# Second attention of a two-layer gated block: scores from the raw context through folded query-key weights, two query tiles on the row halves of TensorE

## What is computed

```python
q = jnp.einsum('bld,de->ble', query, Wq) + bq      # query: 4 x 256 x 128, layer-normalised x
k = jnp.einsum('bld,de->ble', key, Wk) + bk        # key = ctx_512: 4 x 512 x 64, Wk: 64 x 128
v = jnp.einsum('bld,de->ble', value, Wv) + bv      # value = ctx_512
scores = jnp.einsum('bqe,bke->bqk', q, k)
attn = jax.nn.softmax(scores, axis=-1)
out = jnp.einsum('bqk,bke->bqe', attn, v)
...
x = x + jnp.tanh(g_xattn[1]) * out
x = x + jnp.tanh(g_ffn[1]) * _L1_ffn_ref(_layernorm(x, axis=-1), ...)
```

## Time and profile before

| what | value |
|---|---|
| median of the three timed runs | 331.62 us |
| time of the profiled execution | 333.15 us |
| its span | 331.4 us |
| PE busy | 314.9 us, 95% |
| DVE, ACT, POOL busy | 220.3, 193.9, 115.4 us |
| PE's share of the chain that ended last | 74% |

### The profile page before, as it was taken

One profiled execution on the slowest core, in us unless ns is written; L12 is line 12 of the kernel. 1 busy time (PEld: TensorE's weight loads), 2 busy tenths in 40 slices (PEclk: granted clock), 3 DMA queues, 4 the chain that ended last, 5 costly groups with the idle time before them and its releaser, 6 DMA issues.

```text
span 331.4 us, 7484 instructions
## 1 busy us (share of the span) xinstructions
PE 314.9 (95%) x2899; PEld 189.5 (57%) x2899; DVE 220.3 (66%) x531; ACT 193.9 (59%) x410; POOL 115.4 (35%) x200
## 2 busy tenths in 40 slices
PE   8999999999999999899989999999997999999995
PEld 3545734344444434344577677777894467676665
DVE  4998899898989889676352143332322857679665
ACT  3468588989988898787368533333346356422221
POOL 6376723246334333231685004434342301110000
PEclk9999999999999999999999799999999999999999
DMA  7956994661337006150351580000003000000101
GB/s 173 213 106 163 178 211 115 141 168 52 135 115 209 5 3 193 52 146 2 92 179 36 140 212 11 26 13 28 15 18 113 25 2 0 3 0 0 32 3 32
DMA packets 35827, 27.83 MB, mean 84 GB/s; under 512 B 5627, under 2 KB 33070, under 8 KB 35792
## 3 DMA queue, kind: packets, MB, share of 16 engines
q1 hardware_dynamic: 33965, 25.04, 29.6%
q0 software_dynamic: 1280, 1.88, 1.8%
q10 hardware_dynamic: 547, 0.44, 0.5%
HBM read 11.89 MB, written 5.26 MB: 52 GB/s over the span
## 4 chain that ended last, share of the span: by engine, by line
PE 74%; ACT 6%; DVE 6%; POOL 5%; issue 4%; DMA 2%; SPq 1%; DVEq 0%; POOLq 0%; ACTq 0%
PE psum L1881 12%; PE psum L1683 12%; PE psum L1962 8%; PE psum L1624 5%; PE psum L1648 5%; PE psum L1950 4%; PE psum L1869 4%; ACT qk_r L949 2%; POOL rows_in L798 2%; PE psum L1651 2%; PE psum L2065 2%; PE psum L2057 1%; ACT parts L949 1%; PE psum L1701 1%; PE psum L1819 1%
## 5 line engine op out<-in xcount | busy, mean ns | idle before, releaser
L1212 DVE TENSOR_REDUCE nmax<-psum 128x2 f32<-128x1024 f32 (+2 forms) x88 | 101.9, 1214 | 11.0 <-PE psum L1624 9.7
L949 ACT ACTIVATE parts<-psum 128x512 f32<-128x512 f32 (+1 forms) x88 | 45.2, 566 | 8.6 <-PE psum L1648 7.7
L1881 PE MATMUL psum<-p_more,kcat 128*128 128x320 f32 (+2 forms) x160 | 41.9, 408 | 0.9 <-DVE p_more L1345 0.7
L820 POOL DMA_INDIRECT rows_back<-qcat,back_at x24 | 22.9, 953 | 47.8 <-ACT qcat L982 41.8
L1881 PEld LDWEIGHTS psum<-p_more,kcat 128*128 128x128 f32 x160 | 26.9, 195 | 9.9 <-issue 2.2
L1349 DVE TENSOR_TENSOR qcat<-psum,qk_r 128x320 f32<-128x320 f32 (+2 forms) x40 | 16.7, 422 | 22.8 <-ACT qk_r L990 22.7
L990 ACT ACTIVATE qk_r<-psum 128x320 f32<-128x320 f32 (+2 forms) x40 | 15.3, 384 | 25.6 <-PE psum L1881 24.3
L1683 PE MATMUL psum<-parts,v_aug 128*18 128x256 f32 (+1 forms) x352 | 28.5, 369 | 0.0
L1962 PE MATMUL psum<-h_t,kcat 128*128 128x512 f32 x60 | 28.1, 594 | 0.0
L1683 PE MATMUL psum<-qk_r,v_aug 128*18 128x256 f32 (+1 forms) x160 | 27.4, 373 | 0.0
L1028 ACT ACTIVATE qk_r<-psum 128x512 f32<-128x512 f32 x15 | 9.0, 597 | 30.1 <-PE psum L1962 30.1
(11 more groups left out here) (248 smaller groups left out, 621.4 us busy)
## 6 DMA issues: line engine op xcount, KB each, us to landing
kcat<-parts SPq DMA_DIRECT2D x18, 192.0 KB, 3.8
qcat<-parts SPq DMA_DIRECT2D x21, 128.0 KB, 3.7
kcat<-ones_b SPq DMA_DIRECT2D x8, 192.0 KB, 4.0
kcat<-in_L_ffn_wi_gate_dram SPq DMA_DIRECT2D x6, 256.0 KB, 4.2
kcat<-in_L_ffn_wi_up_dram SPq DMA_DIRECT2D x6, 256.0 KB, 4.5
kcat<-in_L_ffn_wo_dram SPq DMA_DIRECT2D x6, 256.0 KB, 5.7
parts<-in_L_ffn_w_dram SPq DMA_DIRECT2D x3, 512.0 KB, 5.5
rows_in<-zeros SPq DMA_DIRECT2D x1, 1290.0 KB, 6.0
```

Source lines behind the costliest of these rows:

```text
L820: pool.indirect_dma_start(out=rows_back[:, :], out_offset=bass.IndirectOffsetOnAxis(ap=back_at[0:m, e, t:t + 1], axis=0), in_=eo[0:m, e % ...
L949: act.activation(p_slots[u % NPT][:, 0:w], s2_bank(s2_place[u])[:, 0:w], ACT.Exp, scale=SCALE).then_inc(p_in, 1)
L1212: dve.tensor_reduce(dst[:, :, n * g:n * (g + 1)], src.rearrange("p (r q k) -> p r q k", r=PAR, q=n), AX.X, ALU.max, negate=True).then_inc( ...
L1881: ins = pe.matmul(gate_up_bank(i, m)[:, 0:end - first], w_t[e][:, m, f * P:(f + 1) * P], xs_t[:, e % 2, first:end], start=True, stop=True)
```

## The change

The scores are no longer made from keys. With `M = Wq Wk'` (128 x 64) a score is `(x M + Wk bq)` times the raw context row, plus an offset `x Wq bk + bq bk` that is the same for a whole row of scores. The row offset does not alter the softmax, but the kernel does keep it: it goes through the DVE step that makes the exponential's bias. The values are computed as they were. What the edit does, in the order of the program:

- the four key products and their four ACT copies are gone; PE turns `w1_q` and `w1_k`, ACT copies the result, PE makes `mk` (the folded 64 columns, one column of query bias for each half of the partitions, one offset column), ACT copies it; the value products stand around these; eight `unread` products follow them, and three more follow the first turn of the routed experts' rows
- SP copies `c_t` from partitions 0-63 to 64-127 (512 KB), behind the loads of the experts' rows and ahead of the loads of layer 1's expert weights
- queries are made 64 wide, an even tile on partitions 0-63 and an odd one on 64-127; one product of 128 by 1 per tile makes the offsets
- the scores of a batch's two tiles are two products of 64 rows, one on each half of the array, issued together; the loop goes by batch and no longer by tile
- DVE has one more small instruction behind each maximum, in two of the steps it waits for the offsets; ACT has three small copies more
- after the first scores three `unread` products stand ahead of the transposes

```diff
-        c_t = sb("c_t", [DC + 1, NC * P])
+        c_t = sb("c_t", [P, NC * P])
...
-        k1_t = q_place(AFTER_HH + 6 * D, NC * P)
+        AFTER_EO = AFTER_HH + 6 * D
+        w1_turned = q_place(AFTER_EO, D + DC + 1)
+        bq_wide = q_place(AFTER_EO + 256, D)
+        MK_BIAS, MK_OFF = DC + 1, DC + 2
+        mk = q_place(AFTER_EO + 384, MK_OFF + 1)
...
+            sp.wait_ge(kv1_full, B)
+            sp.dma_start(c_t[DC:2 * DC, :], c_t[0:DC, :]).then_inc(ctx_again, 16)
...
             def max1(t):
                 dve.wait_ge(sc1_full, t + 1)
-                dve.tensor_reduce(s1_nmax[:, t:t + 1], bank(t % 2), AX.X, ALU.max, negate=True).then_inc(nm1_in, 1)
+                link(dve.tensor_reduce(s1_nmax[:, t:t + 1], bank(t % 2), AX.X, ALU.max, negate=True))
+                if t in (first for first, _ in BACK):
+                    dve.wait_ge(off1_in, [first for first, _ in BACK].index(t) + 1)
+                dve.scalar_tensor_tensor(out=s1_bias[:, t:t + 1], in0=s1_nmax[:, t:t + 1], scalar=s1_off[:, t:t + 1],
+                                         in1=s1_off[:, t:t + 1], op0=ALU.subtract, op1=ALU.add).then_inc(nm1_in, 1)
...
+            def fold_weights_qk():
+
+                pe.wait_ge(mk_act, 1)
+                pe.wait_ge(bq_in, 1)
+                pe.wait_ge(wt_in[0], W_LAST[MK_BANK] + 1)
+                wq, wk, dst = w1_turned[:, 0:D], w1_turned[:, D:D + DC + 1], bank(MK_BANK)
+                pe.matmul(dst[:, 0:DC + 1], wq, wk, start=True, stop=True)
+                for t in range(QT):
+                    pe.matmul(dst[t * DC:(t + 1) * DC, MK_BIAS:MK_BIAS + 1], wk[:, 0:DC], b1_col[:, :], start=True, stop=True)
+                pe.matmul(dst[:, MK_OFF:MK_OFF + 1], bq_wide, wk[:, DC:DC + 1], start=True, stop=True).then_inc(mk_full, 1)
...
-            for j in range(2 * B):
-                context(j)
+            turn_weights_qk()
+            context(0)
+            fold_weights_qk()
+            for b in range(1, B):
+                context(b)
+            unread(N_UNREAD_ROWS)
...
-                pe.matmul(bank(Q1_BANK)[:, 0:(end - first) * P], w1_q[:, :], h_t[:, first * P:end * P],
-                          start=True, stop=True).then_inc(q1_full, 1)
-
-            def scores1(t):
-                pe.wait_ge(q1_act, next(s + 1 for s, (first, end) in enumerate(BACK) if t < end))
+                for t in range(first, end):
+                    dst = bank(Q1_BANK)[t % QT * DC:(t % QT + 1) * DC, (t - first) // QT * P:((t - first) // QT + 1) * P]
+                    ins = pe.matmul(dst, mk[:, 0:DC], h_t[:, t * P:(t + 1) * P], start=True, stop=True)
+                ins.then_inc(q1_full, 1)
+
+            def offsets1(s):
+                first, end = BACK[s]
+                if s == 0:
+                    pe.wait_ge(wt_in[1], E)
+                for t in range(first, end):
+                    ins = pe.matmul(bank(OFF1_BANK[s])[:, t - first:t - first + 1], h_t[:, t * P:(t + 1) * P], mk[:, DC:DC + 1],
+                                    start=True, stop=True)
+                ins.then_inc(off1_full, 1)
+
+            def scores1(b):
+                pe.wait_ge(q1_act, next(s + 1 for s, (first, end) in enumerate(BACK) if QT * b < end))
+                if b == 0:
+                    pe.wait_ge(ctx_again, 16)
+                else:
+                    pe.wait_ge(p1_in, QT * b)
+                for t in range(QT * b, QT * b + QT):
+                    half = slice(t % QT * DC, (t % QT + 1) * DC)
+                    pe.matmul(bank(t % 2), q1_t[half, b, :], c_t[half, b * SC:(b + 1) * SC],
+                              start=True, stop=True).then_inc(sc1_full, 1)
```

More of the change, by code:

```diff
@@ L219, in flamingo_gated_kernel @@
         v1 = q_place(AFTER_HH + 6 * D + NC * P, NC * D).rearrange("p (t d) -> p t d", t=NC)
-        q1_t = qk[:, :, SC:SC + BANK]
-        def q1_of(first, end):
-            return q1_t[:, first // (BANK // P), first % (BANK // P) * P:first % (BANK // P) * P + (end - first) * P]
+        q1_t = qk[:, 0, SC:SC + B * P].rearrange("p (b q) -> p b q", b=B)
         raw1 = raw1_f.rearrange("p (e m d) -> p e m d", e=E, m=3)
@@ L1498, in _ @@
             statistics(2, 2, x_sb)
[L1499 to L1507, removed]
+            max1(1)
+            normalise(2, 2, x_sb)
+            for b in range(B):
+                if b + 1 < B:
+                    max1(QT * (b + 1))
+                    max1(QT * (b + 1) + 1)
+                if b == 2:
                     normalise(3, 0, x1_sb)
-            add_values(NT - 1)
+                reciprocal1(b)
+                add_values(QT * b)
+                add_values(QT * b + 1)
             dense_experts()
@@ L1919, in routed_experts @@
                 transpose_rows(0)
+                unread(N_UNREAD_FIRST)
                 for e in range(E - 1):
@@ L2016, in _, with unread, turn_weights_qk @@
-            for j in range(2 * B):
-                context(j)
+            def unread(n, place=0):
+                for _ in range(n):
+                    pe.matmul(bank(place), ones_b[:, 0:P], ones_b[:, 0:BANK], start=True, stop=True)
+            def turn_weights_qk():
+                dst = bank(TURN1_BANK)
+                pe.transpose(dst[:, 0:D], w1_q[:, :], ident[:, :])
+                pe.transpose(dst[:, D:D + DC + 1], w1_k[:, :], ident[0:DC + 1, 0:DC + 1]).then_inc(mk_full, 1)
+            def fold_weights_qk():
[7 more added lines that the diff above has]
+                pe.matmul(dst[:, MK_OFF:MK_OFF + 1], bq_wide, wk[:, DC:DC + 1], start=True, stop=True).then_inc(mk_full, 1)
@@ new lines, in context @@
+            def context(b):
+                if b == B - 1:
+                    pe.wait_ge(kv1_act, 1)
+                else:
+                    pe.wait_ge(wt_in[0], W_LAST[V1_BANK[b]] + 1)
+                for c in range(CT):
+                    tok = (CT * b + c) * P
+                    ins = pe.matmul(bank(V1_BANK[b])[:, c * P:(c + 1) * P], c_t[0:DC + 1, tok:tok + P], w1_v[:, :],
+                                    start=True, stop=True)
+                ins.then_inc(kv1_full, 1)
+            turn_weights_qk()
@@ L2028, in turn_weights1 @@
                 ins.then_inc(tr_full[1], 1)
-            def unread(n):
-                for _ in range(n):
-                    pe.matmul(bank(0), ones_b[:, 0:P], ones_b[:, 0:BANK], start=True, stop=True)
             def turn_back(s):
```

148 lines of the change are left out of this document (87 added, 61 removed).

## The result

The changed kernel is slower: median 333.52 us (22 runs, 331.57 to 335.60) against 331.84 us (22 runs) for the kernel before timed beside it, ratio 1.005 with a 95% interval of 1.003 to 1.007. The forecast was 331.3 us, and 333.52 lies outside its range.

A forecast was written before the change was run, and what follows sets the result against it. PE was taken to bound most of the chain, with the first expert's row load arriving alongside it in the context stage. Context stage 0 and second attention -0.3 from the 331.62 us median gave 331.3 us, range 329.4 to 332.8.

The forecast's parts named there:

- The context stage: PE work up to the first expert's rows: 3.48 us removed, 3.57 added, so gain 0, at best 0.2 us.
- The reading of the median: Clock fall ahead of the experts, 1.73 us in the profiled run before, does not happen in a typical run.
- E: Rival: clock falls in the new gap behind the second attention's first scores, up to 1.7 us more, 333.0 us; chance 0.09.
- B: Rival: the median run holds the context-stage clock fall and the change removes it, 1.7 us less, 329.6 us; chance 0.27.
- C: Rival: second attention's offset products nearly free, or a wait shorter than read, 0.7 us less, 330.6 us; chance 0.10.
- D: Rival: 32-bit score products on row halves do not overlap, 1.74 us a pair, 1.5 us more, 332.8 us; chance 0.10.
- The walk of the second attention: Step-by-step timing from first scores to dense units: 0.25, say 0.3 us gained, with 0.6 us doubt either way.
- the period: Second attention's loop per batch: set by latency, 4.29 us against 4.40 before, with PE idle 0.5 us a batch.
- the tail: End of the second attention: dense units start 6.65 us after the last batch's scores.
- The DVE step: Second attention: an added instruction between each tile's maximum and exponential, 0.20 us each.

The follow-up runs named there:

- before, wait and small products: Kernel before, with a 0.83 us wait ahead of the second key product, then four unread products of the folding's shapes; median 334.21 us, ratio 1.0057.
- before, with a wait: Kernel before, with the second key product waiting for ACT's copy of the first, nothing folded; median 332.75 us, ratio 1.0018.

## Why the prediction was wrong, by its own steps

**The context stage: this step failed.** It reads "Sum: 0, and -0.2 us at best" and "the stage ends where it did". As a sum of work it was nearly right: at full clock the rows are turned at 184.98 us, forecast 184.6, before 184.52, and the experts start 0.46 us later than before. The same step contains "a wait for ACT ... about 0.8 us"; it was 0.63. I priced the wait by its length and never asked what it does to the clock, though I had read the fall of the earlier trace rows behind an idle stretch. With the wait among small products, 18 of 28 runs are low where the kernel before had about one of six. In the profiled run the fall costs 3.10 us instead of 1.73, since it lasts 6.8 us instead of 3.4 and lies over the last value products and eight unread ones. On the mean of the runs the changed kernel is 1.75 us longer (333.81 against 332.06, without the run of 495.96). Its 14 low runs are on average 2.37 us above its eight at full clock (334.67 and 332.30), which is 1.5 us over all 22; less some 0.2 for the low runs of the kernel before, the rest, about 0.4, is there at full clock too, like the 0.46 us above. That the medians differ by nearly the same 1.68 is chance: a median between two heaps depends on which heap is larger. With the wait filled or gone, no run of 24 is low and the kernel is level with before.

**The reading of the median was right.** "The median does not contain it": the kernel before is low in few runs, and they take 1.5 to 1.8 us longer (medians 333.51 and 331.70 of one set of 29 runs).

**Rivals.** E named the mechanism, at the wrong place. At its own place, behind the first scores, the clock stayed at 1.00 in the profiled run. Its chance of 0.09 was for that place; no rival had a fall behind the new wait of the context stage. B had the sign the wrong way round: the clock was disturbed more often and not less. Its argument, that unread products keep the clock up, holds for this kernel (12 of 12 and 11 of 11 low without the eleven) but is not enough: with them 18 of 28 are low. C is refuted: four offset products took 0.81 us (272.40 to 273.21), priced at 0.85, and the walk was short and not long. (By the Trainium skill, TensorEngine Tiling (Array Packing), Instruction Overhead, where a product of one column has the latency of 60, the estimate for the four was 0.2; the trace does not agree.) D is refuted: 1.06 us a pair, priced at 1.08.

**The walk of the second attention** had the right structure, a loop set by latency, and was 0.6 us short: 5.65 us to the second batch's scores (5.44), 5.94 to the third's (5.70), 4.41 for the period (4.29), 6.73 for the tail (6.65). "The period is latency, 4.29 against 4.40" came out as no gain. Counted from the first turned rows, 259.02 before and 257.75 after at full clock, the dense units follow after 24.51 and 24.60 us: +0.1 instead of -0.3. The gain of the row halves is real, and the offset took it back. The DVE step was priced at 0.20 and takes 0.22, but stands twice in every link of the loop: 1.46 us in all, and the offset products another 0.78. Without either the stage takes 20.48 us, against 22.27 before.

**Still open.** Which combination of wait, small products and following work brings the clock down. (The Trainium skill, TensorE: Matmul & The Clock Gate, What's actually happening, says that the gate runs free of the kernel, so that the same kernel changes its clock at different points; that runs of one program differ agrees with it, but no run here could set that phase.) One unread product in the wait (3 of 6), one-column products moved (2 of 11) and the copy in the kernel before (2 of 6) do not settle it. Nor is it known why the fall lasts 3.4 us in one run and 6.8 in another. Both kernels also have runs at full clock that are over 1 us longer than most (332.98 to 333.19 for the changed one); the profiled run of "before, wait and small products" is one, and there PE is already late when it reaches the context stage. They do not come from the change; their cause is open.

## What to carry to other kernels

Price a new wait on TensorE twice, by its length and by what stands around it: 0.63 us among small products cost little itself, but through the clock it came with 1.6 to 3.8 us more in two runs of three; three products that nobody reads, or the same work placed where its input is ready, removed that. Take the mean granted clock of every run before comparing medians. Before carrying a term through a latency loop for exactness, see whether it cancels: the row offset cost 2.2 us and changed nothing.

## What was unexpected of the hardware

The granted clock fell at about 182 us, when PE had been busy without a gap since the folding began at 179.59, and it stayed at 0.50 to about 188.8 though PE was busy all that time. Falls last 3.4 us in the profile of the kernel before, 6.8 in the changed one, and 13.6 in that of "before, with a wait". The same program falls in some runs and not in others, with its timeline equal to within 0.1 us up to that point. And 32-bit products of 64 rows on the two row halves overlap: 1.06 us for a pair, where one product of 128 rows holds PE for 0.87 and the same pair on one half takes 1.88.
